# Order of steps at the end of the second layer: the second group's scores and mixings moved behind the first group's output products and norm

## The reference, cut to what matters

```python
x = x + L0(gn(x))                      # convolutions with gates
x = x + L1(gn(x))                      # attention over channels
x = x + L2(gn(x))                      # 3x3 and 1x1 convolution
x = x + L3(gn(x))                      # attention over pixels
# L1:
keys = softmax(Wk x + bk, pixels); queries = softmax(Wq x + bq, channels); values = Wv x + bv
context = keys @ values.T
eff = Wr (context.T @ queries) + br
att = sum over x and two differences of blurs L:  softmax(softmax(L, pixels) @ L.T, channels)
out = w0 * eff + w1 * (att.T @ queries)
# gn(v): mean and variance over two channels and all pixels; (v - m) / sqrt(s + 1e-5)
```

## Time and profile before

| What | Value |
|---|---|
| Median of three runs | 310.94 us (the other undisturbed one 310.22) |
| The profiled execution's own time | 310.58 us |
| Its span, first to last instruction | 308.0 us, so 2.58 us lie around it |
| Mean granted TensorE clock | 0.887 of full speed |
| PE / DVE / ACT / POOL busy | 232.2 / 194.8 / 131.0 / 35.9 us |
| The section at hand | 137 us (end of the mixings of the first group) to 197 us (start of the loop of the fourth layer) |

### The profile page before, as it was taken

One profiled execution on the slowest core, in us unless ns is written; L12 is line 12 of the kernel. 1 busy time (PEld: TensorE's weight loads), 2 busy tenths in 40 slices (PEclk: granted clock), 3 DMA queues, 4 the chain that ended last, 5 costly groups with the idle time before them and its releaser, 6 DMA issues.

```text
span 308.0 us, 5530 instructions
## 1 busy us (share of the span) xinstructions
PE 232.2 (75%) x2032; PEld 141.4 (46%) x2032; DVE 194.8 (63%) x533; ACT 131.0 (43%) x322; POOL 35.9 (12%) x64
## 2 busy tenths in 40 slices
PE   0476997464599869989745378739998998997963
PEld 0355654133274754979622122223564463563541
DVE  3672343537279794797977125576497698686772
ACT  1026579100065577794700022236665565641510
POOL 1750000000100100000011502129001011000000
PEclk9999799755599999997965599997999999997995
DMA  6900000000000000000009990454025025000000
GB/s 223 405 4 3 0 3 0 0 0 2 0 0 0 3 0 0 3 0 2 1 10 228 216 213 5 106 128 108 3 52 124 0 50 135 27 17 20 2 34 34
DMA packets 9642, 16.67 MB, mean 54 GB/s; under 512 B 1936, under 2 KB 8208, under 8 KB 9360
## 3 DMA queue, kind: packets, MB, share of 16 engines
q1 hardware_dynamic: 8848, 13.75, 16.3%
q10 hardware_dynamic: 768, 2.58, 4.0%
HBM read 4.87 MB, written 1.05 MB: 19 GB/s over the span
## 4 chain that ended last, share of the span: by engine, by line
PE 50%; DVE 26%; issue 7%; ACT 5%; DMA 5%; POOL 4%; ACTq 2%; SPq 0%; DVEq 0%; POOLq 0%
PE psum L663 7%; PE psum L518 5%; PE psum L691 4%; DMA region<-xn_pad 4%; PE psum L709 4%; PE psum L681 3%; DVE xn_pad L1136 3%; PE psum L643 3%; DVE smax L1142 3%; POOL small L1464 2%; PE psum L479 2%; PE psum L564 2%; PE psum L414 2%; PE psum L506 2%; PE psum L625 2%
## 5 line engine op out<-in xcount | busy, mean ns | idle before, releaser
L1399 ACT ACTIVATE region<-psum 128x512 f32<-128x512 f32 x32 | 19.0, 594 | 30.8 <-PE psum L691 30.7
L1142 DVE TENSOR_REDUCE smax<-psum 128x8 f32<-128x512 f32 x32 | 21.9, 685 | 12.3 <-PE psum L681 12.3
L1464 POOL TENSOR_TENSOR small<-small 128x4 f32<-128x4 f32 x8 | 8.1, 1018 | 175.4 <-DVE small L808 175.4
L663 PE MATMUL psum<-region,w 128*32 128x512 f32 x160 | 23.0, 647 | 4.1 <-DVE region L1117 4.1
L1393 ACT ACTIVATE region<-region 128x512 f32<-128x512 f32 x32 | 20.1, 627 | 12.8 <-DVE region L1149 12.8
L790 DVE BATCH_NORM_STATS2 small<-X 128x6 f32<-128x256 f32 x32 | 12.5, 422 | 17.5 <-ACT X L1269 16.5
L691 PEld LDWEIGHTS psum<-const,region 128*128 128x128 f32 x128 | 14.3, 145 | 17.8 <-issue 11.8
L1149 DVE TENSOR_TENSOR region<-psum,smax 128x512 f32<-128x512 f32 x32 | 22.1, 690 | 0.6
L691 PE MATMUL psum<-const,region 128*128 128x128 f32 x128 | 21.2, 289 | 1.1 <-ACT region L1399 1.0
L709 PE MATMUL psum<-region 128*64 128x18 f32 x512 | 20.5, 214 | 0.0
L709 PEld LDWEIGHTS psum<-region 128*64 128x64 f32 x512 | 17.4, 137 | 5.2 <-issue 5.2
(11 more groups left out here) (169 smaller groups left out, 490.9 us busy)
## 6 DMA issues: line engine op xcount, KB each, us to landing
region<-v_pad SPq DMA_DIRECT2D x64, 80.0 KB, 2.1
region<-xn_pad SPq DMA_DIRECT2D x16, 157.5 KB, 6.8
region<-xn_pad ACTq DMA_DIRECT2D x16, 157.5 KB, 6.6
weight<-weight_in SPq DMA_DIRECT2D x1, 1376.0 KB, 12.6
const<-const_in SPq DMA_DIRECT2D x1, 1330.0 KB, 9.9
X<-x SPq DMA_DIRECT2D x4, 256.0 KB, 5.2
out<-xn_pad SPq DMA_DIRECT2D x8, 128.0 KB, 1.7
weight<-weight_in SPq DMA_DIRECT2D x1, 918.0 KB, 6.7
```

The source lines that it names most:

```text
L663: last = mm(bank(n)[32 * c:32 * c + 32, :], w4[:, c % 2, dx, :], v4[:, j % 2, c, :, :, dx:dx + W], start=(dx == 0), stop=(dx == 4), tile_p ...
L1142: v.tensor_reduce(smax[:, w, :], src, X_AXIS, ALU.max).then_inc(smax_ready, 1)
L1399: a.activation(e3T[:, u % NE, :], bank(where[("e3T", u)]), ACT.Copy).then_inc(e3T_ready, 1)
```

## The change

Three steps of the second group are taken out of the list and put in at later places: scores of the first pair goes to just ahead of ("norm", 2, 0), scores of the second pair and mixing of the first pair go to just ahead of ("mix", 1, 1).

```diff
+for moved, before in ((("scores1", 0, 1), ("norm", 2, 0)), (("scores1", 1, 1), ("mix", 1, 1)), (("mix", 0, 1), ("mix", 1, 1))):
+    SCHEDULE.remove(moved)
+    SCHEDULE.insert(SCHEDULE.index(before), moved)
 del SCHEDULE[SCHEDULE.index(("het", 0, 0)):]
```

## The result

| | Before | After |
|---|---|---|
| Median | 311.18 us (16 runs) | 312.89 us (16 runs) |
| Ratio to before, 95% interval | 1 | 1.0056 [1.0033, 1.0079] |
| The profiled execution | 310.58 us, span 308.0 | 312.01 us, span 310.2 |
| Mean granted clock | 0.887 | 0.873 |

The changed kernel is slower by 0.56%, 1.7 us: less than 2%, but the interval of the ratio does not reach 1. The forecast was 312.0 us, 1.4 us over the profiled execution of before.

A forecast was written before the change was run, and what follows sets the result against it. DMA engines were taken to set the pace from 160.2 us, with the first group's norm setting the stretch's end. 310.58 us - 0.3 (rows) + 1.7 (clock) gave 312.0 us, range 307.5 to 315.5 us.

The forecast's parts named there:

- Steps 1 to 4: First group's output products, adds, then queries, scores and norm: norm ready at 152.4 us against 160.18, 7.8 us earlier.
- The late clock: TensorE stays at half clock through the second group's first-pair scores, norm at 156.7, total 316.3 us; chance 0.13.
- Step 5: ACT's eight DMA issues behind the first norm, 6.11 us, hold the last pair's query copy and six softmaxes until 162.1.
- The first rival: ACT is not held by its DMA issues, which run beside its compute; 308.0 us, without clock loss 306.3; chance 0.15.
- Step 6: DVE stops 4.0 us for ACT ahead of the last mixing; second group's norm at 172.6 us against 170.47, 2.1 later.
- Step 7: Second group's rows have the DMA engines to themselves, 14.05 us: in at 186.6 us against 186.92, 0.3 us gained.
- Step 8: TensorE at the second group's rows, at half clock after 8.6 us of little work: 1.7 us lost.

The follow-up runs named there:

- e7_before_warm: Kernel before plus six unread matmuls, three behind the first group's last convolution, three ahead of the wait for the second group's rows; 312.49 us, ratio 1.0062.
- e6_both_scores_first: Changed kernel with scores of both second-group pairs ahead of the first group's norm, only the first pair's mixing behind it; 309.47 us, ratio 0.9904.
- e4_warm: Changed kernel plus six unread matmuls, three behind the first group's last convolution, three ahead of the wait for the second group's rows; 310.93 us, ratio 0.9987.
- e1_act_late: Changed kernel with ACT issuing the first group's eight row DMAs behind the softmaxes of the second group's last pair; 308.81 us, ratio 0.9907.
- e5_late_warm: Changed kernel with both ACT's eight first-group DMAs behind the last pair's softmaxes and the six unread matmuls; 305.85 us, ratio 0.9784.

## Why the prediction was right

**Steps 1 to 4, the first norm.** Forecast 7.8 us earlier, 11.1 us behind the start of the mixing row (152.4 - 141.32); measured 151.48 - 140.41 = 11.07. The late clock, the slower rival, did not come: the four matmuls that turn this pair's queries took 0.60 us (line 585 at 142.56 us).

**Step 5, ACT held by its issues.** Right, and the step on which the whole forecast turned. Eight issues took 6.49 us, 6.11 were expected, and the copy starts 0.04 us behind the last. The first rival would have been 4 us faster; the row of 8, 4 and 0 issues decides against it. The Trainium skill's page "DMA: Bandwidth & Descriptors" (section "Issuing engines are not separate DMA queues") calls the sequencer's time usually small relative to the DMA. Here it is not small: for the second group's rows ACT's eight issues take 6.87 of the 13.91 us from the first issue (171.94) to the convolution that waits for them (185.85), and for the first group's the 6.49 us held ACT's copy and softmaxes; the measurement decides.

**Step 6, DVE's gap.** 4.0 expected, 4.64 measured: 0.4 of the difference are the longer issues, the rest is that DVE was through with the first mixing 5.4 us behind the first norm (156.90 us) and not 5.7. The second norm was expected 31.3 us behind the mixing row, and came 31.49 behind it. The 7.8 us gained in front (18.86 us behind the mixing row before, 11.07 after) are more than lost between the norms: 10.3 us before, 20.4 after.

**Step 7, the rows.** 14.05 us expected from the norm to the convolution, 13.95 measured, and 13.9 to 14.1 in every kernel but before, e7_before_warm and e6_both_scores_first; before it was 16.4. In e6_both_scores_first (14.6) the first group's rows are issued latest of the changed kernels. From the mixing to the convolution 45.3 expected, 45.44 measured: 0.16 us gained, 0.3 in the forecast.

**Step 8, the clock.** Right in kind, a little small in size: 1.7 us expected, 2.15 measured (convolution to fourth layer 12.60 us against 10.45), 2.49 by e4_warm. I had taken one half-clock stretch of before, 3.3 us, for the price; here half clock lasted from ahead of the rows to past 189 us. The reason that step 8 gives, the longer stretch of little work (8.6 us expected, 7.57 measured, against 4.6), is not shown. Unread matmuls in the stretch kept the clock up in three kernels, so little work there is part of it. But in e6_both_scores_first the stretch is 4.95 us and the clock fell all the same. Each kernel has one profile only (that one took 311.05 us, the median is 309.47), so it is open what decides at this length, and whether it is the same in every execution.

**The sum.** +1.4 us forecast; +1.99 in the profiles up to the fourth layer, +1.7 by the ratio. So the gain of the moved steps was there, 7.8 us at the first norm, and it was given back twice: to ACT's list, and to TensorE's clock. Each term is right to within 0.8 us. That the profiled execution took 312.01 us against a forecast of 312.0 is luck: the changed kernel's was 0.91 us ahead at the mixing row, took 1.12 us more from the start of the fourth layer on and 0.77 us less outside the span, and none of the three was in the forecast.

## What to carry to other kernels

When one list orders all engines, moving a step moves its DMA issues too, and an engine that computes pays for them with everything behind them: count the issues by their length in the trace, and put them behind the work that somebody waits for, or on an engine that does nothing else. An earlier start of a transfer can be worth nothing if the producer of the next transfer gets later by it (here 7.8 us at the first norm became 0.16 us at the rows); follow the last transfer, not the first. And where work is pulled away from in front of a wait, look at the clock behind the wait, but count the idle time there before filling it.

## What the runs showed of the hardware that was not expected

A DMA issue in ACT's list does not wait for the activations ahead of it to finish: in e1_act_late the first issue starts at 153.66 us, while softmaxes that stand ahead of it in the list still start until 154.64. In the changed kernel the copy behind eight issues started 0.04 us after the last of them. So an issue holds what is behind it, and not what is ahead.

The same instructions up to the end of the first group's mixings took from 137.75 to 142.51 us in the eleven profiles. The longest low stretch of the clock lies ahead of this point: between 55 and 95 us the granted clock was 0.74 in e5_late_warm, the kernel with the earliest mixing, and 0.66 in all ten others. These three lines are of before, after and e5_late_warm, in this order, from three answers:

```profile
55.00:95.00 40.00, 25.81 (x99) 15.18 (x100) 22.54 (x64) 7.67 (x22) 1.04 (x1) 0.66 0.00 0
```

```profile
55.00:95.00 40.00, 26.86 (x101) 15.66 (x102) 22.74 (x66) 7.05 (x19) 1.04 (x1) 0.66 0.00 0
```

```profile
55.00:95.00 40.00, 27.38 (x107) 15.50 (x107) 24.55 (x66) 9.40 (x26) 1.04 (x1) 0.74 0.00 0
```

So this clock may bear on e5_late_warm's early mixing, but not on the spread of the ten others, from 139.84 to 142.51 us; where that comes from stays open. The spread is why no difference of a microsecond or two should be read from two spans alone.
